# Two-layer macaron block on one core: the second layer's mix two slots later, its normalised and transposed input made at the head of the phase

## The reference, cut to what matters

```
x = u + 0.5 * ffn(LN(u))        # first layer
x = x + attn(LN(x))             # the mix
x = x + 0.5 * ffn(LN(x))        # second layer, same weights
ffn(x)  = silu(x Ws_up) Ws_down + sum over 64 experts of cw[t,e] * (silu(x W_up[e]) W_down[e])
cw      = sigmoid(affinity) of the top 8 of (x centroids^T + bias), divided by its sum, else 0
attn(u) = gamma*(xf + xb) + (1-gamma)*u ;  xf, xb = u WB^T, u WBf^T with the first / last token kept
gamma   = sigmoid(xf w1 + xb w2 + b)
```

## Time and profile before

| what | value |
|---|---|
| median of three runs | 767.62 us |
| profiled execution, device time | 767.55 us |
| span of its trace | 765.7 us |
| TensorE matmuls (PE) busy | 752.7 us, 98% |
| VectorE, ScalarE, GpSimd busy | 82%, 83%, 72% |
| granted TensorE clock | full speed in all slices |
| chain of waits, share of the span | PE 65%, ACT 12%, DVE 10%, issue 5%, POOL 5%, DMA 2% |
| one 512-column matmul in the profile | 390 ns long, one started every 227 ns |

### The profile page before, as it was taken

One profiled execution on the slowest core, in us unless ns is written; L12 is line 12 of the kernel. 1 busy time (PEld: TensorE's weight loads), 2 busy tenths in 40 slices (PEclk: granted clock), 3 DMA queues, 4 the chain that ended last, 5 costly groups with the idle time before them and its releaser, 6 DMA issues.

```text
span 765.7 us, 11535 instructions
## 1 busy us (share of the span) xinstructions
PE 752.7 (98%) x3359; PEld 613.7 (80%) x3359; DVE 627.3 (82%) x1390; ACT 635.1 (83%) x1224; POOL 554.7 (72%) x583
## 2 busy tenths in 40 slices
PE   8999999999999999999999999999999999999998
PEld 5787878887888878888788887888888878888886
DVE  6788988969889687887878878887797978979775
ACT  7999868888699886988879798888988879788785
POOL 3795768676888777877777867778688686886553
PEclk9999999999999999999999999999999999999999
DMA  8000001121011101011010111101111010111000
GB/s 295 15 1 28 9 15 34 29 36 27 15 36 42 48 14 39 9 41 48 14 41 21 27 48 27 27 21 35 28 28 29 21 44 7 28 34 28 15 2 14
DMA packets 69446, 25.23 MB, mean 33 GB/s; under 512 B 55713, under 2 KB 68257, under 8 KB 69409
## 3 DMA queue, kind: packets, MB, share of 16 engines
q1 hardware_dynamic: 69408, 24.79, 12.7%
HBM read 9.05 MB, written 2.10 MB: 15 GB/s over the span
## 4 chain that ended last, share of the span: by engine, by line
PE 65%; ACT 12%; DVE 10%; issue 5%; POOL 5%; DMA 2%; DVEq 0%; ACTq 0%; POOLq 0%; SPq 0%
PE y_ps L1123 11%; PE y_ps L1125 10%; PE y_ps L1124 10%; PE up L1123 10%; PE up L1125 10%; PE up L1124 10%; ACT g_hi L738 4%; ACT up L701 4%; POOL g_lo L466 3%; DVE gated L947 2%; DVE g_lo L956 2%; DMA n_turned_halves<-n_halves 2%; DVE up L947 2%; ACT normed L821 2%; PE side L1183 1%
## 5 line engine op out<-in xcount | busy, mean ns | idle before, releaser
L466 POOL TENSOR_TENSOR g_lo<-gated,g_hi 128x512 fp32r<-128x512 f32 x255 | 332.7, 1305 | 149.0 <-ACT g_hi L738 148.2
L701 ACT ACTIVATE up<-up 128x512 f32<-128x512 f32 x512 | 299.9, 586 | 68.3 <-PE up L1125 66.9
L947 DVE TENSOR_TENSOR gated<-up,cw 128x512 f32<-128x512 f32 x256 | 175.3, 685 | 80.1 <-ACT up L701 76.5
L1123 PE MATMUL y_ps<-g_hi,wd_hi 128*128 128x512 f32 x512 | 203.2, 397 | 3.8 <-POOL g_lo L466 2.6
L947 DVE TENSOR_TENSOR up<-up,cw 128x512 f32<-128x512 f32 x256 | 177.1, 692 | 31.3 <-ACT up L701 29.5
L1123 PE MATMUL up<-x_hi,wu_hi 128*128 128x512 f32 x512 | 200.2, 391 | 0.8 <-DVE g_lo L956 0.6
L1125 PE MATMUL y_ps<-g_hi,wd_lo 128*128 128x512 f32 x512 | 199.6, 390 | 0.0
L1124 PE MATMUL y_ps<-g_lo,wd_hi 128*128 128x512 f32 x512 | 199.5, 390 | 0.0
L1125 PE MATMUL up<-x_hi,wu_lo 128*128 128x512 f32 x512 | 199.4, 389 | 0.0
L1124 PE MATMUL up<-x_lo,wu_hi 128*128 128x512 f32 x512 | 199.3, 389 | 0.0
L956 DVE TENSOR_TENSOR g_lo<-up,g_hi 128x512 fp32r<-128x512 f32 x256 | 174.6, 682 | 11.7 <-ACT g_hi L738 10.5
(11 more groups left out here) (163 smaller groups left out, 559.0 us busy)
## 6 DMA issues: line engine op xcount, KB each, us to landing
x_in<-in_x SPq DMA_DIRECT2D x8, 256.0 KB, 2.7
wu_raw<-in_w_up SPq DMA_DIRECT2D x4, 512.0 KB, 7.9
wd_raw<-in_w_down SPq DMA_DIRECT2D x4, 512.0 KB, 8.6
x_res<-in_x SPq DMA_DIRECT2D x8, 256.0 KB, 2.7
out<-out_sb SPq DMA_DIRECT2D x7, 256.0 KB, 2.2
mix<-in_mix SPq DMA_DIRECT2D x1, 389.0 KB, 7.4
n_turned_halves<-n_halves SPq DMA_TRANSPOSE x19, 2.7
out<-out_sb SPq DMA_DIRECT2D x2, 128.0 KB, 1.9
```

Source lines behind the costliest of these rows:

```text
L466: nc.gpsimd.tensor_tensor(g_lo[:, i, :], gated[:, t // 2 % ORING, :], g_hi[:, i, :].bitcast(fp32), ALU.subtract).then_inc(lo_done[1], 1)
L701: nc.scalar.activation(up[i][:, :], up[i][:, :], ACT.Silu).then_inc(silu_done, 1)
L947: nc.vector.tensor_tensor(gated[:, t // 2 % ORING, :] if t % 2 else up[i][:, :], up[i][:, :], cw[ph.q][:, :], ALU.mult).then_inc(gate_done, 1)
L1123: nc.tensor.matmul(o, a[0], b[0], start=start, stop=False)
```

## The change

In B's table the mix stands about two slots later: `u_pack` 15, 17 becomes 16, 17; `u_join` 19, 21 becomes 20, 22; `edge` 22 becomes 24; `attn` and `edge_add` 25 become 27; `tanh` and `gamma` 26 become 28; `x2` 27, 28 becomes 30, 31. ScalarE's `sig` moves from 15 to 17. Norm 2 of the batch whose x2 lies in `x2_mid` leaves the end of phase B (slots 29 to 34) for its head: `stat2` 0, 1, `aggr2` 2, `rstd2` 3, `norm2` 5, 6, `x2_pack` 8, 9, and `x2_join` comes from slots 3 and 5 of the next phase A to slots 13 and 14 of phase B. In A's table `x_split` moves from 7 to 4. SyncE issues `turn_x2` ahead of `turn_u`. The number of instructions in a turn of the loop is the same.

Around the loop: phase 1 moves the affinity steps by two slots and the mix by one or two, `norm2` and `x2_pack` go from its slots 33, 34 to slots 1 to 4 of phase 2, where the join goes from 3, 5 to 8, 9 and the affinity steps from 11 to 14. Phase 13 gets a table of its own, `AT_THIRTEEN`: mix and norm 2 as in the old B, the join that stood in slots 33, 34 of phase 12 in its slots 1, 2, `x_split` at 3 in place of 1, `aff` at 8 in place of 4. Phase 14 keeps the old join and split.

```diff
--- before.py
+++ after.py
@@ -76,32 +76,41 @@
 }
 AT_SECOND = {
     "both_high": 1, "both_low": 5,
-    "stat0": (0, 1), "aggr0": 2, "rstd0": 3, "shift0": 4, "norm0_act": (6, 7), "x_t": 10, "x_copy": 10, "x_split": 11,
-    "aff": 15, "aff_pack": 15, "sh_silu": 16, "sh_high": 17, "sh_low": 18, "aff_join": 17,
-    "bias": 19, "sig": 19, "max": 20, "take": 21, "gate": 23, "sum": 24, "inv": 25, "cw_pack": (26, 27), "cw_join": (31, 32),
-    "y": 2, "y_t": 5, "x1": 6, "stat1": (8, 9), "aggr1": 10, "rstd1": 11, "norm1": (13, 14), "xu": 19, "u_t": 20,
-    "u_copy": 20, "edge": 21, "edge_sum": 22, "attn": 24, "edge_add": 25, "tanh": 25, "gamma": 25, "x2": (27, 28),
-    "stat2": (29, 30), "aggr2": 30, "rstd2": 31, "norm2": (33, 34), "x2_pack": (33, 34),
+    "stat0": (0, 1), "aggr0": 2, "rstd0": 3, "shift0": 4, "norm0_act": (6, 7), "x_t": 11, "x_copy": 11, "x_split": 12,
+    "aff": 17, "aff_pack": 17, "sh_silu": 18, "sh_high": 19, "sh_low": 20, "aff_join": 19,
+    "bias": 21, "sig": 21, "max": 22, "take": 23, "gate": 24, "sum": 25, "inv": 26, "cw_pack": (27, 28), "cw_join": (32, 33),
+    "y": 2, "y_t": 5, "x1": 6, "stat1": (8, 9), "aggr1": 10, "rstd1": 11, "norm1": (13, 14), "xu": 20, "u_t": 22,
+    "u_copy": 22, "edge": 23, "edge_sum": 25, "attn": 25, "edge_add": 27, "tanh": 27, "gamma": 27, "x2": (29, 30),
+    "stat2": (31, 32), "aggr2": 32, "rstd2": 34,
     "mix": 2,
 }
 AT_THIRD = {
-    "y": 2, "x2_join": (3, 5), "x_split": 7,
-    "aff": 11, "aff_pack": 11, "sh_silu": 12, "sh_high": 13, "sh_low": 15, "aff_join": 13,
-    "bias": 16, "sig": 17, "max": 18, "take": 19, "gate": 21, "sum": 22, "inv": 23, "cw_pack": (24, 25), "cw_join": (29, 31),
-    "stat0": (1, 2), "aggr0": 3, "rstd0": 5, "shift0": 6, "norm0_act": (16, 18), "x_pack": (20, 22), "x_join": (33, 34),
-    "y_t": 6, "x1": 8, "stat1": (9, 10), "aggr1": 11, "rstd1": 12, "norm1": (13, 14), "xu": 18, "u_t": 20,
-    "u_copy": 20, "edge": 23, "edge_sum": 24, "attn": 25, "edge_add": 26, "tanh": 27, "gamma": 27, "x2": (29, 30),
+    "y": 2, "norm2": (1, 2), "x2_pack": (3, 4), "x2_join": (8, 9), "x_split": 10,
+    "aff": 14, "aff_pack": 14, "sh_silu": 15, "sh_high": 16, "sh_low": 18, "aff_join": 16,
+    "bias": 19, "sig": 19, "max": 20, "take": 21, "gate": 23, "sum": 24, "inv": 25, "cw_pack": (26, 27), "cw_join": (31, 32),
+    "stat0": (3, 4), "aggr0": 5, "rstd0": 6, "shift0": 8, "norm0_act": (16, 18), "x_pack": (20, 22), "x_join": (33, 34),
+    "y_t": 6, "x1": 8, "stat1": (9, 10), "aggr1": 11, "rstd1": 12, "norm1": (13, 14), "xu": 18, "u_t": 21,
+    "u_copy": 21, "edge": 23, "edge_sum": 25, "attn": 25, "edge_add": 26, "tanh": 27, "gamma": 27, "x2": (29, 30),
     "keep": 9, "roll": 32,
 }
 AT_STEADY_A = {
-    "y": 2, "x2_join": (3, 5), "x_split": 7, "y_join": (9, 11), "sum_out": 17, "keep": 19, "roll": 27,
+    "y": 2, "x_split": 4, "y_join": (9, 11), "sum_out": 17, "keep": 19, "roll": 27,
     "aff": 11, "aff_pack": 11, "sh_silu": 12, "sh_high": 13, "sh_low": 15, "aff_join": 13,
     "bias": 16, "sig": 17, "max": 18, "take": 19, "gate": 21, "sum": 22, "inv": 23, "cw_pack": (24, 25), "cw_join": (29, 31),
     "stat0": (8, 9), "aggr0": 10, "rstd0": 11, "shift0": 14, "norm0_act": (16, 18), "x_pack": (20, 22), "x_join": (33, 34),
 }
 AT_STEADY_B = {
     "x_split": 1, "aff": 4, "aff_pack": 4, "sh_silu": 5, "sh_high": 6, "sh_low": 12, "aff_join": 9,
-    "sig": 15, "bias": 15, "max": 16, "take": 18, "gate": 20, "sum": 21, "inv": 23, "cw_pack": (24, 25), "cw_join": (29, 31),
+    "sig": 17, "bias": 15, "max": 16, "take": 18, "gate": 20, "sum": 21, "inv": 23, "cw_pack": (24, 25), "cw_join": (29, 31),
+    "y": 2, "y_join": (5, 7), "x1": 7, "stat1": (8, 9), "aggr1": 10, "rstd1": 10, "shift1": 13, "norm1_act": (14, 15),
+    "xu": 23, "u_pack": (16, 17), "u_join": (20, 22),
+    "attn": 27, "edge": 24, "edge_sum": 26, "edge_add": 27, "tanh": 28, "gamma": 28, "x2": (30, 31),
+    "stat2": (0, 1), "aggr2": 2, "rstd2": 3, "norm2": (5, 6), "x2_pack": (8, 9), "x2_join": (13, 14),
+}
+
+AT_THIRTEEN = {
+    "x2_late_join": (1, 2), "x_split": 3, "aff": 8, "aff_pack": 8, "sh_silu": 9, "sh_high": 10, "sh_low": 13, "aff_join": 11,
+    "sig": 17, "bias": 16, "max": 17, "take": 19, "gate": 20, "sum": 21, "inv": 23, "cw_pack": (24, 25), "cw_join": (29, 31),
     "y": 2, "y_join": (5, 7), "x1": 7, "stat1": (8, 9), "aggr1": 10, "rstd1": 10, "shift1": 13, "norm1_act": (14, 15),
     "xu": 23, "u_pack": (15, 17), "u_join": (19, 21),
     "attn": 25, "edge": 22, "edge_sum": 24, "edge_add": 25, "tanh": 26, "gamma": 26, "x2": (27, 28),
@@ -109,8 +118,9 @@
 }
 
 AT_TWELVE = {k: v for k, v in AT_STEADY_A.items() if k not in NORM0}
-AT_TWELVE.update({"roll": 20, "stat2": (22, 24), "aggr2": 25, "rstd2": 25, "norm2": (27, 28), "x2_pack": (29, 30), "x2_late_join": (33, 34)})
+AT_TWELVE.update({"roll": 20, "stat2": (22, 24), "aggr2": 25, "rstd2": 25, "norm2": (27, 28), "x2_pack": (29, 30)})
 AT_FOURTEEN = {k: v for k, v in AT_STEADY_A.items() if k not in NORM0 + ("roll",)}
+AT_FOURTEEN.update({"x2_join": (3, 5), "x_split": 7})
 AT_LAST = {
     "y": 2, "y_t": 6, "out": 7, "keep": 11,
 }
@@ -120,14 +130,14 @@
 
     phase(Phase(0, 0, AT_FIRST, prep=(0, 0, 1), norm0=1, first=True))
     phase(Phase(1, 1, AT_SECOND, mid=0, norm2=0, prep=(1, 0, 2), norm0=2))
-    phase(Phase(2, 0, AT_THIRD, mid=1, prep=(1, 2, 0), keep=0, norm0=3))
+    phase(Phase(2, 0, AT_THIRD, mid=1, norm2=0, prep=(1, 2, 0), keep=0, norm0=3))
     with eng.Fori(2, B - 2) as c:
         phase(Phase(2 * c - 1, 1, AT_STEADY_B, mid=c, norm2=c - 1, prep=(c, 0, c + 1), use=c - 1))
         phase(Phase(2 * c, 0, AT_STEADY_A, post=c - 2, prep=(c, 2, c - 1), keep=c - 1, norm0=c + 2, use=c))
     c = B - 2
     phase(Phase(2 * c - 1, 1, AT_STEADY_B, mid=c, norm2=c - 1, prep=(c, 0, c + 1)))
     phase(Phase(2 * c, 0, AT_TWELVE, post=c - 2, norm2=c, prep=(c, 2, c - 1), keep=c - 1))
-    phase(Phase(2 * c + 1, 1, AT_STEADY_B, mid=c + 1, norm2=c + 1, prep=(c + 1, 2, c)))
+    phase(Phase(2 * c + 1, 1, AT_THIRTEEN, mid=c + 1, norm2=c + 1, prep=(c + 1, 2, c)))
     phase(Phase(2 * c + 2, 0, AT_FOURTEEN, post=c - 1, prep=(c + 1, 2, c + 1), keep=c))
     phase(Phase(2 * c + 3, 1, AT_LAST, post=c, keep=c + 1))
 
@@ -404,9 +414,9 @@
                 turn_aff(2 * c - 1)
                 load_x(c + 2)
                 load_res(c + 1)
+                turn_x2(c - 1)
                 turn_u(c)
                 turn_weights(2 * c - 1)
-                turn_x2(c - 1)
                 turn_y(2 * c)
                 turn_aff(2 * c)
                 store(c - 2)
@@ -577,9 +587,13 @@
                     if t in ph.at.get("x_join", ()):
                         join_x(0, ph.at["x_join"].index(t), x_moved, 16 * (ph.norm0 - 2), ph.norm0 - 1)
                     if t in ph.at.get("x2_join", ()):
-                        join_x(1, ph.at["x2_join"].index(t), x2_moved, 16 * (ph.prep[2] + 1), ph.prep[0] + 1)
+                        if ph.u_dma:
+
+                            join_x(1, ph.at["x2_join"].index(t), x2_moved, 16 * (ph.norm2 + 1), ph.prep[0] + 1)
+                        else:
+                            join_x(1, ph.at["x2_join"].index(t), x2_moved, 16 * (ph.prep[2] + 1), ph.prep[0] + 1)
                     if t in ph.at.get("x2_late_join", ()):
-                        join_x(0, ph.at["x2_late_join"].index(t), x2_moved, 16 * (ph.norm2 + 1), ph.prep[0] + 1)
+                        join_x(0, ph.at["x2_late_join"].index(t), x2_moved, 16 * (ph.prep[2] + 1), ph.prep[0])
                     if t in ph.at.get("x2_pack", ()):
                         h = ph.at["x2_pack"].index(t)
                         pack(n_halves, h, norm_done[2], blocks_of(normed[2][:, :, :], h), ph.norm2 + 1, x2_packed)
```

## The result

The changed kernel takes 769.96 us (median of eight runs, 769.64 to 770.58), the one before 767.56 beside it (766.91 to 767.64): ratio 1.0034, interval 1.0025 to 1.0044. Slower by 2.4 us, where 3.8 less were forecast.

A forecast was written before the change was run, and what follows sets the result against it. TensorE, busy 98% of the span, was taken as the floor, with only its delays to win. Terms 2.0 - 0.16 + 1.8 - 0.3 + 0.45 = 3.8 us off 767.55 gave 763.8 us; range 759.6 to 767.4.

The forecast's parts named there:

- `sig` and `u_join` (tiles 15 and 19): Phase B: `sig` behind slot 15 gains 0.64 us at tile 15, `u_join` behind slot 20's low part 0.47 at tile 19.
- later mix, new narrow places: Phase B: `attn` two slots later takes cover from tiles 20 and 21; 0.1 us lost per B phase.
- the head with its first half, and the packs: B's head: stats and first `norm2` half covered by idle time; packs ahead of tile 9's low part lose 0.05 us.
- second half beside GpSimd: B's head: second `norm2` half, meeting GpSimd's low part of tile 5, delays up tile 11; 0.75 us lost.
- `rstd2` off tile 31's path: End of B: norm 2 leaving slots 29 to 34 frees tile 31's low part; 0.30 us gained per turn.
- The port term: B's head: `norm2` and GpSimd share ports, whichever issues first blocks the other; 0.75 us lost, ceiling 2.9.
- rival 2: B's head: `norm2` held in both halves makes gate 7 later, B over 48.5 us; 770 us in all, chance 0.14.
- Phase 11: Last B phase of the loop's kind: 0.74 us of delay removed, 0.90 lost, so 0.16 slower.
- The failed step around the loop: Phases 1 and 2: 1.8 us gained, 0.3 lost to moved steps; phases 12 and 13: 0.45 gained.
- Rival 3: Slots 14 to 20 of B: ScalarE is the pace, delays return at tiles 17, 19 or 21; 766.9 us, chance 0.16.
- Rival 1: B's head: the port costs little, `norm2` at slot 6 slips between GpSimd's instructions; 759.8 us, chance 0.20.

The follow-up runs named there:

- e5: The kernel before with one number of B's table changed, `sig` from slot 15 to 17 (phase 13 keeps the old table): 762.74 us, ratio 0.9944.
- e6: e5 plus the later mix in B, norm 2 staying in slots 29 to 34: 763.92 us, ratio 0.9961.
- e9: The kernel before with `sig` at 17 and norm 2 at B's head, both `norm2` halves in slot 5, old mix: 762.57 us, ratio 0.9949.
- e4: The changed kernel with both halves of `norm2` in slot 5 of B instead of slots 5 and 6: 766.91 us, ratio 0.9997.
- e7: The kernel before with only norm 2 moved to B's head (`norm2` in slots 5, 6), old mix and `sig`: 770.81 us, ratio 1.0047.
- e2: The kernel before with only the change's part of phases 1 and 2: 768.09 us, ratio 1.0014.
- e3: The kernel before with only phase 13's new table, the join in its slots 1, 2: 768.38 us, ratio 1.0018.
- e12: e3 with x1 of phase 13 in slot 8 instead of 7 and its stats one slot later: 767.51 us, ratio 1.0006.
- e11: e2 with `x2_join` at 7, 8 and `x_split` at 9 in phase 2, one slot earlier: 768.12 us, ratio 1.0015.
- e10: The changed kernel with both halves of `norm2` in slot 6 of B: 772.39 us, ratio 1.0069.
- run 680: Not a run label: 680 ns is the mean length of `w_sel` over the whole run of e6.

## Why the prediction was wrong, step by step

Terms in us per turn of the loop, plus is slower; measured is the difference of the stretches of the kernels named:

| term | forecast | measured | from |
|---|---|---|---|
| `sig` and `u_join` (tiles 15 and 19) | -1.11 | -0.94 | e5 against before |
| later mix, new narrow places | +0.10 | +0.18 | e6 against e5, B |
| the head with its first half, and the packs | +0.05 | +0.24 | e9 against e5, B |
| second half beside GpSimd | +0.75 | +0.85 | changed kernel against e4, B |
| `rstd2` off tile 31's path | -0.30 | -0.37 | e9 against e5, A |
| sum | -0.51 | -0.04 | trace: -0.06 |

- *The port term* was right in place, cause and size (gate 7 at 263.95 for 264.00, 0.69 for 0.75).
- *The failed step inside the loop* is the size of four terms, not their adding up. Measured one by one they sum to the trace's value within 0.02, and the head costs as much with the old `sig` (e7: 1.12) as with the new (0.24 and 0.85). The stalls removed were worth 0.17 less than I took, the later mix cost 0.08 more, the port 0.10 more, and the rest of the head's edits 0.24, where I had taken nothing but the packs' 0.05 because the engines idle there. Tile 15 has next to no slack in these kernels (0.03 us in e4), so small latenesses ahead of it, which no bracket shows, count too. I had written that VectorE is nearly full from slot 7 to 14 "so lateness isn't made good", for rival 2, and did not put it into the forecast. Four turns: 1.8 us of the miss.
- *`u_join`* is a wrong cause with nearly the right size: tile 19 was repaired by `sig`.
- *Phase 11*: forecast +0.16, measured +0.78. Its `sig` gain is 0.60 (e5), and the second half in slot 6 costs it 1.03 (47.99 against e4's 46.96); the mix (0.15, e6) and the rest of the head (0.23, e9) make up the rest.
- *The failed step around the loop is the larger*: phases 1 and 2 at 1.5 faster are 1.07 slower, phases 13 and 14 at 0.45 faster are 1.35 slower; 4.4 of the 6.7 us between forecast and trace. The gains were sized well (1.65 of 1.8, and the whole 1.0 of phase 13). What failed is the price of the moved steps, 0.3 and nothing: I did not follow join and split through GpSimd's queue to what then stands behind them (`y_join` and x1 in phase 13, the product of slot 14 in phase 2, by way of `cw_join` that of slot 4 in phase 3), nor the shared expert's low part to the transposes behind it. New waits of 1.4 and 1.3 in phases 1 and 2, 0.8 in phase 3, and 0.4, 0.7 and 0.76 in phases 13 and 14 took the place of those removed. That these moves cost is shown by e2 and e3, that it goes through x1 in phase 13 by e12, through `x_lo` in phase 2 by e11; the transposes of phase 1, phase 3 and tile 31 of phase 14 are read from the traces alone. Phases 1 and 2 came out just past the far end of my bounds (0.5 gained less 1.5), phase 13 far outside of its own (0 to 1.0 gained).
- *Rivals.* None came out whole. Rival 2 gave 770 by a held first half; in the changed kernel both blocks of the first half take 0.34, and B is 47.90, not over 48.5. That the time is rival 2's is chance: it had the phases around the loop 1.95 faster. Rival 3 named the right manner, delays that come back since ScalarE is the pace, and the size of the loop, but not the loss around it. Rival 1's cheap port is excluded by e4 and e10.

## What to carry to other kernels

A removed stall is worth its length only if nothing else on the engines between was made later by the same edit: price the chain up to the next slack, small latenesses without a bracket included, and not the row alone. Where two stalls lie some tiles apart, look first whether the second is the first one's echo; one number (`sig` 15 to 17) took both for 4.3 us, and the larger rearrangement lost it all. When an edit moves work in an engine's queue, list what is queued behind its new place, and put VectorE work that GpSimd can hold where GpSimd waits: here the same two blocks, issued 0.3 us behind a low part instead of ahead of it, cost 0.85 us a phase.

## What the runs showed of the hardware that was not expected

- More VectorE instructions are held beside GpSimd than the layer norm's block: `w_sel` lasts 1.19 us and `w_norm` 1.24 in phase 5 instead of 0.42 and 0.47, and x1 1.74 in phase 13 instead of 0.68. With the mix two slots later `w_sel` fell beside a low part and `w_norm` beside `xu` (means over the run 680 and 727 ns in e6, 442 and 434 in e5). The forecast had used only what the Trainium skill (SBUF — State Buffer, "Who interferes with whom") says of tensor_scalar; it also says that a VectorE instruction with two inputs in SBUF contends with a GpSimd one that reads SBUF. The traces agree: all three have two such inputs.

```profile
282.88 1.19 DVE L938 SCALAR_TENSOR_TENSOR w_sel<-taken,sig 128x256 f32<-128x256 f32 x1
...
287.67 1.24 DVE L952 SCALAR_TENSOR_TENSOR w_norm<-w_sel,w_inv 128x256 f32<-128x256 f32 x1
```

- The same four blocks cost 1.11 us ahead of GpSimd (e4) and 2.51 behind it (e10), and GpSimd, when second, only 0.12 (1.42 for 1.30).
- After a wait of TensorE the second matmul starts 0.30 to 0.35 behind the first instead of 0.23 (265.59 and 265.93 in the changed kernel): 0.1 us on top of each stall read here.
